# Graph attention on one core: a pair's weighted sums in four steps of one chunk, in place of three steps

## The reference

```python
def gat_layer(x, adj, W, a_self, a_neigh, b):
    feat = jnp.einsum('nf,hfo->hno', x, W)
    attn_self = jnp.einsum('hno,ho->hn', feat, a_self)
    attn_neigh = jnp.einsum('hno,ho->hn', feat, a_neigh)
    e = attn_self[:, :, None] + attn_neigh[:, None, :]
    e = jax.nn.leaky_relu(e, LRELU_ALPHA)
    e = e + MASK_VAL * (1.0 - adj)[None, :, :]
    alpha = jax.nn.softmax(e, axis=-1)
    out = jnp.einsum('hnm,hmo->hno', alpha, feat) + b[:, None, :]
    out = jnp.transpose(out, (1, 0, 2)).reshape(out.shape[1], -1)
    return jax.nn.elu(out)

def per_graph(x, a):
    h = gat_layer(x, a, W0, a_self0, a_neigh0, b0)
    return gat_layer(h, a, W1, a_self1, a_neigh1, b1)
...
x = x + _L0_xattn_ref(ctx_512, _layernorm(x, axis=-1), ...)
```

## Time and profile before

| | |
|---|---|
| median of 3 runs | 2141.94 us (2138.0 to 2146.16) |
| the profiled execution | 2139.37 us, span 2137.6 us |
| TensorE, VectorE busy over the span | 84%, 66% |
| ScalarE, GpSimd busy over the span | 50%, 41% |
| graph attention | 0 to about 560 us |
| windows 115 to 187 us | TensorE busy 64.8, VectorE 59.8, ScalarE 60.8, GpSimd 50.0 us of 72 |

### The profile page before, as it was taken

How to read it: one execution, slowest core, us unless ns; L and a number is a source line. 1 busy time by engine, 2 the same in 40 slices (tenths; PEclk the granted TensorE clock), 3 DMA queues, 4 the chain that set the end, 5 groups by cost and what they waited for, 6 DMA issues and landing times. The chain is left out here.

```text
span 2137.6 us, 32682 instructions
## 1 busy us (share of the span) xinstructions
PE 1795.9 (84%) x9679; PEld 1025.0 (48%) x9679; DVE 1406.1 (66%) x2807; ACT 1062.3 (50%) x2149; POOL 881.9 (41%) x949
## 2 busy tenths in 40 slices
PE   4689877998548999999993279999997539999997
PEld 2344443444334555555551123333332538888885
DVE  5887877788684666566553478888883765545543
ACT  5588877878332333333332347777776412222222
POOL 5476676668103545555542311111111014444442
PEclk8699988999768999999996579999999759999998
DMA  5111211111455889889655752222221718999993
GB/s 148 55 40 40 83 62 55 40 46 35 147 152 126 177 189 236 224 196 230 122 103 157 158 103 62 57 69 56 62 64 44 267 42 221 230 235 234 230 236 58
DMA packets 202146, 272.01 MB, mean 127 GB/s; under 512 B 83484, under 2 KB 121852, under 8 KB 200956
## 3 DMA queue, kind: packets, MB, share of 16 engines
q1 hardware_dynamic: 156315, 166.52, 25.9%
q0 software_dynamic: 38544, 97.02, 22.5%
q10 hardware_dynamic: 7121, 6.44, 1.6%
HBM read 200.25 MB, written 69.17 MB: 126 GB/s over the span
## 5 line engine op out<-in xcount | busy, mean ns | idle before, releaser
L2074 DVE TENSOR_REDUCE a_negmax<-a_m 128x2 f32<-128x1024 f32 x256 | 304.2, 1221 | 97.2 <-PE a_m L1938 97.2
L291 POOL TENSOR_TENSOR g_near<-g_mask,g_tb 128x512 f32<-128x512 f32 x256 | 322.5, 1282 | 100.0 <-DVE g_emin L545 99.1
L2023 ACT ACTIVATE a_prob<-a_s 128x512 f32<-128x512 f32 x512 | 274.3, 595 | 83.4 <-PE a_s L1948 83.3
L1464 PE MATMUL f_gu_bank<-f_wgu,f_xT 128*128 x768 | 265.5, 489 | 2.9 <-ACT f_xT L1512 2.9
L1258 PEld LDWEIGHTS s_gu_bank<-s_xT,s_wgu 128*128 128x128 f32 x2048 | 240.8, 193 | 31.8 <-issue 27.5
L374 PE MATMUL g_pt<-g_ident,g_p 128*128 128x128 f32 x1024 | 173.5, 299 | 87.1 <-DVE g_pT L554 82.1
L1258 PE MATMUL s_gu_bank<-s_xT,s_wgu 128*128 128x128 f32 x2048 | 241.4, 277 | 1.6 <-ACT s_xT L1288 1.6
L1426 POOL DMA_INDIRECT out<-f_y,f_ids x96 | 151.2, 1575 | 209.5 <-DMA out<-f_y,f_ids 167.6
L475 ACT ACTIVATE g_p<-g_e,g_emin 128x512 f32<-128x512 f32 x256 | 183.4, 716 | 96.0 <-DVE g_emin L545 95.2
L374 PEld LDWEIGHTS g_pt<-g_ident,g_p 128*128 128x128 f32 x1024 | 122.3, 150 | 217.5 <-DVE g_pT L554 142.5
L1464 PEld LDWEIGHTS f_gu_bank<-f_wgu,f_xT 128*128 128x128 f32 x768 | 146.3, 191 | 125.8 <-issue 48.6
(11 more groups left out here) (291 smaller groups left out, 2767.2 us busy)
## 6 DMA issues: line engine op xcount, KB each, us to landing
s_wgu<-in_L_ffn_w_gate_up SPq DMA_DIRECT2D x32, 1024.0 KB
f_wgu<-in_L_ffn_gate_up_proj SPq DMA_DIRECT2D x32, 768.0 KB
s_wd<-in_L_ffn_w_down SPq DMA_DIRECT2D x32, 512.0 KB
a_qT<-q_parts SPq DMA_DIRECT2D x217, 64.0 KB, 2.4
g_tb<-neighbours SPq DMA_DIRECT2D x8, 1536.0 KB, 8.0
f_wd<-in_L_ffn_down_proj SPq DMA_DIRECT2D x32, 384.0 KB
q_parts<-p_part SPq DMA_DIRECT2D x48, 128.0 KB, 2.3
g_tb<-neighbours SPq DMA_DIRECT2D x8, 512.0 KB, 4.3
```

The source lines that it names most:

```text
L291: pool.tensor_tensor(near[:, n % LAG, :], mask[slot][:, local % NT, :], t_all[k % SLOTS][:, local // NT, :], ALU.add).then_inc(near_ready, 1)
L1464: last = nc.tensor.matmul(gu_bank[j % TR][:, 0:F], xT[j % TR][:, c, :], wgu_flat[:, bass.ds(place_of[j] + c * F, F)], start=(c == 0), stop ...
L2023: nc.scalar.activation(prob[n][:, :], bank_of("score", G, n)[:, :], ACT.Exp).then_inc(p_ready, 1)
L2074: V.tensor_reduce(negmax[k % RING][:, 2 * half:2 * half + 2, head], m_bank[i % RING][:, :, :], X_AXIS, ALU.max, negate=True).then_inc(m_re ...
```

## The change

One line, the table of steps. The chunks 0, 1, 2, 3 are summed at steps 2, 2, 3, 4 before, and at steps 2, 3, 4, 5 now.

```diff
     STEPS = 3 * PAIR
-    SUMS = {2: range(0, 2), 3: range(2, 3), 4: range(3, 4)}
+    SUMS = {2: range(0, 1), 3: range(1, 2), 4: range(2, 3), 5: range(3, 4)}
     PREP_FIRST, PREP_FEAT, PREP_END = 8, 15, 40
```

## The result

The changed kernel takes 2167.49 us (median of 4 runs, 2163.16 to 2170.33), the kernel before in the same session 2142.14 us (4 runs, 2138.0 to 2146.16). The ratio is 1.0113, with a 95% interval from 1.0097 to 1.0128: slower by 24 us by the ratio and 25 between the medians, where 20 were forecast (2162 us, range 2150 to 2173).

The account below looks back on a forecast made before the run. TensorE and VectorE were taken to wait on each other in the graph attention, closing at L567. Terms 8.0 + 3.2 + 5.8 + 2.4 + 0.7 = 20.1 us on a 2141.94 us median gave 2162 us, range 2150 to 2173.

Parts of the forecast that it names:

- The circle of T(2), last chunk, L567, copy, T(2): Graph attention's loop from step 2's transposes through TensorE's sums and VectorE back to the next such transposes; 13.09 us.
- The plain pair: Pair of heads without projection matmuls between its transposes; 0.73 us longer in each of 11, 8.0 us together.
- The feature pairs: Eight pairs with next phase's projections between transposes; four cost 0.80 us each, four 1.45: 3.2 and 5.8 us.
- Leg: TensorE's way from step 2's transposes to L567; in a feature pair it grows by 1.64 to 9.67 us.
- The L347 pairs: Four pairs with 16-row products between their transposes; 0.14 us of cover, so 2.4 us cost together.
- The pairs with cover: Pairs where L567 is late already, so sums end before it could start; two cost 0.7 us together, six nothing.
- the six pairs: Pairs where VectorE is late with masks and weights; tightest cover 1.30 us, more than 0.73, so no cost.
- The pair at 109.26: Graph attention pair where L567 has 0.38 us of cover; claimed to cost 0.35 us.
- the other one with little cover: Second pair said to be like the one at 109.26; the two cost 0.7 us together.
- The half clock: Rival: TensorE's clock falls once in each of 11 plain pairs, 0.61 us each, 6.7 us added, 2168 us; chance 0.10.
- The cost of the signal: Cost of `pv_done` moving from step 4 to 5, lengthening the way to L567; 0.73 us in a plain pair.
- The batches: Skill's rule for back-to-back matmuls, which speaks against breaking step 2's batch; by the sum it adds nothing.

Follow-up runs that it names:

- e3: Changed kernel with VectorE's L567, L571, L578 and ScalarE's L492 (the operations that read the sums) one step later; 2127.56 us, ratio 0.9933 to the kernel before.
- e4: Kernel before, with VectorE's L567, L571, L578 and ScalarE's L492 one step later, TensorE's order as before; 2131.8 us, ratio 0.9953.
- e1: Kernel before with chunks 0, 1, 2 and 3 summed at steps 2, 3, 4 and 4, last signal still at step 4; 2143.19 us, ratio 1.0002.
- e7: Changed kernel with some transposes made twice in plain pairs to fill TensorE's idle time; 2162.9 us, ratio 1.0076 to the kernel before.
- e5: Kernel before with the new steps in the eight feature pairs only, old steps elsewhere; 2154.5 us against 2144.3, ratio 1.0039.
- e8: Kernel before with some transposes made twice in plain pairs to fill TensorE's idle time; 2135.2 us, ratio 0.9947.
- the filled kernels: e7 and e8: the changed kernel and the kernel before, both with some transposes made twice; 2162.9 and 2135.2 us.
- e11: The changed kernel itself run once more for a second profile, nothing altered; 2168.57 us in the one run.
- e2: Kernel before with the four chunks summed one per step at steps 1 to 4, step 2's waits moved to step 1; 2141.78 us, ratio 0.9996.
- e9: Changed kernel with both the finishing steps one later (e3) and the doubled transposes (e7); 2129.1 us, ratio 0.9937 to the kernel before.

## Why the prediction was right

**What bounds.** The circle of T(2), last chunk, L567, copy, T(2) was the right one. e3 and e4 show it: the same exchange of TensorE's order, the reader moved, and the cost is gone. e1 shows that the first half of the change (the second chunk leaves step 2) is worth nothing in the kernel's time either way, as the forecast had it.

**The plain pair.** Forecast +0.73 us, measured 13.83 against 13.10 at full clock. The wait at L567 was forecast at 1.13 us. At full clock it is 1.09 to 1.21 in the plain pairs that close a phase, and 1.57 in those of the last phase (e7): that is e1's 0.84 and the 0.73. In single pairs it is up to 1.99.

**The feature pairs.** Leg forecast 9.67 us, measured 9.67. Pairs forecast 17.31 and 16.50 us, measured 17.36 and 16.49. e5, these eight alone, cost 8.4 us (3.6 to 12.9) for a forecast of 9.0.

**The L347 pairs.** The wait at L567, forecast about 1.4 us, is 1.39, and between e8 and e7 such a pair grows from 15.84 to 16.43 us, the 0.59 of the forecast.

**The pairs with cover: too cheap.** This term of the sum was mis-sized. "More than 0.73: nothing" measured the cover against a leg that begins at T(2). But in two of the six pairs T(4) itself waits for a copy of the late VectorE, so the 0.86 us that step 2 saves are lost there and the leg behind T(4) grows by a whole T and chunk, 0.58 + 1.01 = 1.59 us. Timeline of TensorE in the tightest of the six, T(4) in the kernel before:

```profile
351.39 0.66 PE L374 MATMUL g_pt<-g_ident,g_p 128*128 128x128 f32 x4 [1.06 <-DVE g_pT L554]
```

and in the changed kernel T(4) and the last chunk, with the L567 behind it:

```profile
363.02 0.66 PE L374 MATMUL g_pt<-g_ident,g_p 128*128 128x128 f32 x4 [1.90 <-DVE g_pT L554]
...
365.92 1.96 PE L404 MATMUL g_o<-g_pT,g_feat 128*64 128x512 f32 x4
```

```profile
368.00 0.70 DVE L567 TENSOR_TENSOR g_o<-g_o,g_rall 128x512 f32<-128x512 f32 x1 [1.80 <-PE g_o L404]
```

T(4) waits 1.90 us, and the last chunk at 365.92 runs at half clock. L567 waits 1.80 us where it had 1.30 us to spare. T(4) starts 20.73 us after the L567 of the pair before in the changed kernel, and 20.74 us in the kernel before: what step 2 saved does not reach it. At full clock the step is 1.59 - 1.30 = 0.29 us; between the filled kernels this pair comes 24.11 us behind the L567 before it, against 23.83. The pair at 109.26 loses most of the saving in the same way, since T(4) now waits 0.39 us in it, and costs 1.03 us where 0.35 were forecast; the other one with little cover costs 0.14 for 0.35. Of the 8 new cases in which L567 waits (28 in place of 20), four are the L347 pairs; the others are two of the six and the two with little cover, 0.34 to 1.80 us each.

**The sum.** The forecast is 20.1 us. Measured are 24 to 25 us in the whole runs, and in the profiles, up to the last L567, 26.8 us (30.0 with e11 in place of the first profile, 24.9 between the filled kernels). To take the half clock out, except where every profile shows it, I take for each pair the shortest distance from L567 to L567 that it shows in the two profiles of the old order (before, e8) and in the three of the new one (after, e7, e11). The two sums are 486.1 and 507.6 us: without the half clock the change costs 21.5 us. That is 1.4 over the forecast, of which 1.0 is the pairs with cover.

**The half clock: a rival that came in part.** What the distances of a profile add up to above these sums, I take as the cost of the half clock: 7.3 us in the kernel before, 12.8 and 15.3 us in the two profiles of the changed kernel, 0.4 in e8 and 3.6 in e7. So in these profiles the half clock adds 3 to 8 us to the cost of the change. The forecast had it at nothing in its sum, and as a rival of 6.7 us; the measured 2167 us is in fact nearer to that rival's 2168 than to the forecast's 2162. Its bound for a plain pair, 0.61 us, was too low: such pairs show up to 1.9 us. The cost of the signal was forecast rightly, and a part of the rival came on top. Where the stretches fall is chance (e11), and five profiles are few, so that the change itself brings more of them is suggested and not shown. (The range given, 2150 to 2173, is also 1 us lower than the bounds it was drawn from, 2151 to 2174.)

**The batches.** The Trainium skill, page "Perfetto Trace Analysis", section "Matmul Optimizations", says that matmuls should come back to back in batches because the engine scales with utilization. e8 agrees (more back-to-back work, granted clock 0.97 for 0.94, 0.53% faster). e2, where the batch is broken into the same four pieces as in the change, shows none of the 25 us (ratio 0.9996), and e1 shows nothing for moving the batch.

## What to carry to other kernels

Evening out an engine's work over the steps doesn't help if it puts off the signal at the end, and a reader that an in-order engine reaches on time passes every delay on to all that is queued behind it: here 0.73 us in a plain pair and 1.44 us where other work lies in between (16.49 for 15.05). Look for the instruction that waits, and then see whether it can stand one step later; that was worth more (15 us under the kernel before in e3, 11 in e4) than any placing of the sums tried here. To cost a wait, look from which point the way to the signal is bound: time saved ahead of another wait is lost. And don't take the waiting time of an instruction for its price: in e1 it grew from 0.40 to 0.84 us in a plain pair while the pair kept its 13.10 us.

## What the runs showed of the hardware

TensorE's clock is at half after a wait of 1.20 us in one pair and at full after one of 1.21 us in another, and where it falls changes from one execution of the same program to the next (e11). A half-clock stretch costs a plain pair up to 1.9 us (15.76 for 13.83). Making three of eight units' transposes twice in the plain pairs, some 1.5 us of added work in a pair of 13 us (an estimate, from 0.44 to 0.58 us for a unit's transposes), went with a granted clock of 0.97 in place of 0.94 over 100 to 560 us and made the kernel 0.53% faster (interval 0.32 to 0.74%). What is to be noticed is that more work was the gain, and that it was gone once most of the wait was (e9 against e3).
